# A graph network on one core: ranking work moved apart, edge sums kept in PSUM, one comparison for seven source one-hots

## The reference

```python
h = relu(layernorm(x))
# two SAGE convolutions, sums over the edges that end in a node
def conv(x, Wl, Wr, b):
    agg = segment_sum(x[src], dst); cnt = segment_sum(1, dst)
    return (agg / max(cnt, 1)) @ Wl.T + b + x @ Wr.T
x = x + conv2(relu(conv1(h)))
h = relu(layernorm(x))
# edge network, mean over the edges that START in a node
e   = relu(concat(h[src], h[dst], edge_attr) @ W1 + b1)
msg = e @ W2 + b2
out = x + segment_sum(msg, src) / max(count(src), 1)
```

## Time and profile before

| | us |
|---|---|
| median of 3 runs | 4867.47 |
| lowest, highest | 4842.37, 4877.82 |
| the profiled execution | 4839.18 |
| its span | 4837.4 |
| VectorE busy | 4073.2 (84%) |
| TensorE matmuls busy | 4006.2 (83%) |
| GpSimd busy | 2251.4 (47%) |
| ScalarE busy | 2068.5 (43%) |

### The profile page before, as it was taken

One profiled execution on the slowest core, in us unless ns is written; L12 is line 12 of the kernel. 1 busy time (PEld: TensorE's weight loads), 2 busy tenths in 40 slices (PEclk: granted clock), 3 DMA queues, 4 the chain that ended last, 5 costly groups with the idle time before them and its releaser, 6 DMA issues. The chain is left out here.

```text
span 4837.4 us, 186125 instructions
## 1 busy us (share of the span) xinstructions
PE 4006.2 (83%) x71043; PEld 3837.8 (79%) x71043; DVE 4073.2 (84%) x9221; ACT 2068.5 (43%) x4806; POOL 2251.4 (47%) x2144
## 2 busy tenths in 40 slices
PE   0788888888888899999946888888888888888886
PEld 0677778777777799999945878888888888888876
DVE  4788888888887688888876989898989898998987
ACT  1455555555554466666633222222223232232222
POOL 0000000000000466666626777777777777777771
PEclk9899999999997799999977999999989899999998
DMA  2121222222221555444414444444454455545441
GB/s 60 38 66 59 67 65 65 65 59 67 65 65 46 146 117 116 116 116 116 117 35 149 152 153 146 153 151 155 156 158 158 158 158 158 158 158 157 155 130 55
DMA packets 429135, 542.34 MB, mean 112 GB/s; under 512 B 136727, under 2 KB 393935, under 8 KB 428452
## 3 DMA queue, kind: packets, MB, share of 16 engines
q1 hardware_dynamic: 359396, 457.21, 31.0%
q0 software_dynamic: 67840, 77.39, 6.5%
q10 hardware_dynamic: 1426, 0.35, 0.0%
HBM read 462.66 MB, written 72.01 MB: 111 GB/s over the span
## 5 line engine op out<-in xcount | busy, mean ns | idle before, releaser
L1258 POOL DMA_INDIRECT sorted_edges<-edge_rows,edge_index x1590 | 1691.5, 1064 | 571.7 <-issue 476.6
L988 ACT CAST conv_rows<-conv_rows_ps 128x384 bf16<-128x384 f32 (+1 forms) x2597 | 1167.3, 449 | 873.7 <-PE conv_rows_ps L908 863.9
L908 PE MATMUL conv_rows_ps<-parts,conv_hot_t 128*128 128x192 bf16 x9328 | 1199.6, 247 | 193.3 <-DVE conv_hot_t L1052 189.9
L925 PE MATMUL conv_sums<-conv_rows,conv_hot_d 128*128 128x193 bf16 (+1 forms) x9328 | 1201.8, 247 | 4.5 <-DMA conv_got<-parts_table,conv_index 4.5
L908 PEld LDWEIGHTS conv_rows_ps<-parts,conv_hot_t 128*128 128x128 bf16 x9328 | 780.4, 98 | 238.7 <-issue 177.6
L925 PEld LDWEIGHTS conv_sums<-conv_rows,conv_hot_d 128*128 128x128 bf16 x9328 | 813.8, 98 | 5.8 <-DMA conv_got<-parts_table,conv_index 5.4
L1322 PE MATMUL edge_sums<-edge_parts,edge_hot 128*128 128x64 bf16 (+1 forms) x15582 | 588.9, 199 | 232.6 <-DVE acc L1484 232.6
L1322 PEld LDWEIGHTS edge_sums<-edge_parts,edge_hot 128*128 128x128 bf16 x15582 | 548.9, 101 | 246.3 <-DVE acc L1484 195.6
L872 POOL MEMSET acc<- 128x6500 f32 x2 | 11.0, 5514 | 1540.6 <-POOLq L440 1540.6
L886 POOL DMA_INDIRECT conv_got<-parts_table,conv_index x530 | 510.3, 963 | 291.8 <-issue 165.7
L1052 DVE TENSOR_SCALAR conv_hot_t<-conv_slot_row,node_of 128x896 bf16<-128x896 bf16 (+2 forms) x1484 | 603.5, 449 | 3.1 <-PE conv_rows_ps L908 0.8
(11 more groups left out here) (174 smaller groups left out, 4659.6 us busy)
## 6 DMA issues: line engine op xcount, KB each, us to landing
conv_slot_row<-slot_rows SPq DMA_DIRECT2D x371, 224.0 KB, 3.2
edge_slot_row<-slot_rows SPq DMA_DIRECT2D x371, 224.0 KB
edge_edges<-sorted_edges SPq DMA_DIRECT2D x371, 224.0 KB
edge_dst_row<-dst_rows SPq DMA_DIRECT2D x265, 192.0 KB
edge_attr<-in_edge_attr SPq DMA_DIRECT2D x260, 192.0 KB
conv_slot_row<-slot_rows SPq DMA_DIRECT2D x212, 192.0 KB
conv_slot_row<-slot_rows SPq DMA_DIRECT2D x159, 160.0 KB, 3.1
sorted_edges<-edge_rows,edge_index POOLq DMA_INDIRECT x1590
```

Of the source, the lines that this page charges most:

```text
L908: mm = pe.matmul(rows_ps[i % banks][:, at:at + PARTS * D], hot_t[(h + g) % 2][:, v, u * P:(u + 1) * P], k.parts[:, 2 * (GU * g + u) + v].r ...
L925: mm = pe.matmul(sums[h][:, v * wide_cols:(v + 1) * wide_cols], hot_d[(h + g) % 2][:, u, v * P:(v + 1) * P], row, start=(i == 0 and u == 0 ...
L988: act.copy(rows[i % bufs][:, 0:n, 0:PARTS * D], rows_ps[i % banks][:, 0:n * PARTS * D].rearrange("p (u d) -> p u d", u=n)).then_inc(copied, 1)
L1258: pool.indirect_dma_start(k.sorted, bass.IndirectOffsetOnAxis(ap=index[h][0:used, at:at + 1], axis=0), rows[j][0:used, t, :], None).then_i ...
```

## The change

1. **Ranking in conv1.** The instructions stay; their places in the lists change. `two_planes` is cut into two calls, one after group 2 as before and one after group 3. `choose` keeps the product after group 4; the sum (`sum_chosen`) goes behind group 5, the spreading of ranks and the first slot comparison behind group 6, and the two other comparisons behind the next block's group 0. On TensorE the first scatter piece stays at step `bs - 1`, the second and third go to steps 1 and 3 of the next block (they were at `bs - 5`, `bs - 3`, `bs - 1`), and `turn` goes from step 4 to 8. On ScalarE `take_slots` goes from step 2 to 6, `take_row` from 5 to `cut - 1`, `take_dst` from `cut - 4` to `cut - 1` (this one in conv2 too), `keep_rank` one step on.
2. **Edge sums.** `total` and `left` are gone. `add_edges`, `rest_of_first` work in place in `a_ps` (PSUM), and ScalarE's two parts and the third part read from there. `expand` waits for the third part of two groups before, where it waited for its `total`. To have a bank free, `attr_ps` has one buffer instead of two, and `turn` waits for the copy of the transpose before.
3. **Source one-hots.** The seven comparisons of `make_hot` become one, of the form that conv has for `hot_d`, with node numbers in PSUM (`nodes_ps`); `src_of` is bf16 with every number four times.

```diff
+def same_number(dve, hot, nodes, number, g):
+    shape = [P, GU, SW // QUAD, QUAD]
+    return dve.tensor_tensor(hot[:].rearrange("p u (n q) -> p u n q", q=QUAD), wide(quads(nodes), 1, shape),
+                             wide(number[:, GU * g:GU * (g + 1), :], 2, shape), ALU.is_equal)
...
 # conv, TensorE, first(b, h, n)
-                        if i == 4 and sorts(b, 1):
+                        if i in (1, 3) and sorts(b, 1):
+                            s.scatter(pe, b + 1, n if n == MANY else n + 1, (i + 1) // 2)
+                        if i == 8 and sorts(b, 1):
                             s.turn(pe, b + 1, n if n == MANY else n + 1)
 # second(b, h, n)
-                    if i in (bs - 5, bs - 3, bs - 1):
-                        s.scatter(pe, c, m, (i - bs + 5) // 2)
+                    if i == bs - 1:
+                        s.scatter(pe, c, m, 0)
...
 # conv, ScalarE
-                    if i == 2 and sorts(b, 1):
+                    if i == 6 and sorts(b, 1):
                         s.take_slots(act, b + 1, n if n == MANY else n + 1)
-                    if i == 5 and sorts(b, 1):
-                        s.take_row(act, b + 1, n if n == MANY else n + 1)
-                    if i == cut - 4 and (not isinstance(b, int) or b + 1 in range(NB)):
-                        take_dst(b + 1, 1 - h, n if n == MANY else n + 1)
                     if i == cut - 2 and sorts(b, 2):
                         s.keep_earlier(act, b + 2, n if n == MANY else n + 2)
+                    if i == cut - 1 and sorts(b, 1):
+                        s.take_row(act, b + 1, n if n == MANY else n + 1)
+                    if i == cut - 1 and (not isinstance(b, int) or b + 1 in range(NB)):
+                        take_dst(b + 1, 1 - h, n if n == MANY else n + 1)
-                    if i == bs - 4 and sorts(b, 2):
+                    if i == bs - 3 and sorts(b, 2):
                         s.keep_rank(act, b + 2)
...
 # conv, VectorE
                 if sorts(b, 2):
-                    s.two_planes(dve, b + 2, h, m)
+                    s.plane(dve, b + 2, h, m, 0)
...
+                    if g == 3 and sorts(b, 2):
+                        s.plane(dve, b + 2, h, m, 1)
                     if g == 4 and sorts(b, 2):
                         s.choose(dve, b + 2, m)
                     if g == 5 and sorts(b, 2):
-                        s.slots(dve, b + 2, m)
+                        s.sum_chosen(dve, b + 2, m)
+                    if g == 6 and sorts(b, 2):
+                        s.spread_rank(dve, b + 2)
+                        s.slots(dve, b + 2, m, 0)
...
                     make_hot(b + 1, 1 - h, n if n == MANY else n + 1, 0)
+                if sorts(b, 2):
+                    for j in range(1, PIECES):
+                        s.slots(dve, b + 2, m, j)
...
 # sum_edges
-                if n >= 1 or j >= 2:
-                    pe.wait_ge(attr_ready, q - 1)
+                if n >= 1 or j >= 1:
+                    pe.wait_ge(attr_ready, q)
...
-                pe.wait_ge(totaled, number + NG - 1)
+                pe.wait_ge(third_made, number - 1 + NG + 1)
...
-                act.activation(parts[at][:, :, 0, 0:D], total[at][:], ACT.Relu).then_inc(first_made, 1)
+                act.activation(parts[at][:, :, 0, 0:D], a_ps[at][:, 0:GU, :], ACT.Relu).then_inc(first_made, 1)
-                act.copy(parts[at][:, :, 1, 0:D], left[at][:]).then_inc(second_made, 1)
+                act.copy(parts[at][:, :, 1, 0:D], a_ps[at][:, 0:GU, :]).then_inc(second_made, 1)
...
-                dve.tensor_tensor(total[at][:], a_ps[at][:, 0:GU, :], edges[g][:], ALU.add).then_inc(totaled, 1)
+                dve.tensor_tensor(a_ps[at][:, 0:GU, :], a_ps[at][:, 0:GU, :], edges[g][:], ALU.add).then_inc(totaled, 1)
-                dve.scalar_tensor_tensor(left[at][:], total[at][:], 0.0, parts[at][:, :, 0, 0:D], ALU.max, ALU.subtract).then_inc(left_made, 1)
+                dve.scalar_tensor_tensor(a_ps[at][:, 0:GU, :], a_ps[at][:, 0:GU, :], 0.0, parts[at][:, :, 0, 0:D], ALU.max, ALU.subtract).then_inc(left_made, 1)
-                for u in range(GU):
-                    dve.tensor_scalar(hot[at][:, u, :], k.nodes_b[:], src_of[h][:, GU * g + u:GU * g + u + 1], None, ALU.is_equal)
+                same_number(dve, hot[at], nodes_ps[:, 0:SW // 2].bitcast(BF16), src_of[h], g)
-                dve.tensor_tensor(parts[at][:, :, 2, 0:D], left[at][:], parts[at][:, :, 1, 0:D], ALU.subtract).then_inc(third_made, 1)
+                dve.tensor_tensor(parts[at][:, :, 2, 0:D], a_ps[at][:, 0:GU, :], parts[at][:, :, 1, 0:D], ALU.subtract).then_inc(third_made, 1)
```

More of the change, by code:

```diff
@@ L619, in members, with plane @@
                           wide(self.number[h][:, 0], 2, shape), ALU.is_equal).then_inc(self.member_made, 1)
-    def two_planes(self, dve, c, h, n):
+    def plane(self, dve, c, h, n, i):
         shape = [P, BT, SRC_COLS // QUAD, QUAD]
-        if n >= 1:
-            dve.wait_ge(self.scattered, c)
-        dve.wait_ge(self.member_made, c + 1)
-        for i in range(2):
-            last = dve.tensor_tensor(self.planes[:, :, i, :].rearrange("p t (n q) -> p t n q", q=QUAD), self.member[:].rearrange("p t (n q) -> p t n q", q=QUAD),
-                                     wide(self.number[h][:, 1 + i], 2, shape), ALU.mult)
-        last.then_inc(self.planes_made, 1)
+        if i == 0:
+            if n >= 1:
+                dve.wait_ge(self.scattered, c)
+            dve.wait_ge(self.member_made, c + 1)
+        made = dve.tensor_tensor(self.planes[:, :, i, :].rearrange("p t (n q) -> p t n q", q=QUAD), self.member[:].rearrange("p t (n q) -> p t n q", q=QUAD),
+                                 wide(self.number[h][:, 1 + i], 2, shape), ALU.mult)
+        if i:
+            made.then_inc(self.planes_made, 1)
     def count(self, pe, c, n):
@@ L955, in first @@
                 else:
+                    for j in range(1, PIECES):
+                        if sorts(b, 1):
+                            s.scatter(pe, b + 1, n + 1, j)
                     s.count(pe, b + 2, n + 2)
@@ L1058, in make_hot @@
                     dve.wait_ge(reduced, number - 1)
-                shape = [P, GU, SW // QUAD, QUAD]
-                nodes = k.nodes_b[:] if sorting else nodes_ps[:, 0:SW // 2].bitcast(BF16)
-                dve.tensor_tensor(hot_d[hot][:].rearrange("p u (n q) -> p u n q", q=QUAD), wide(quads(nodes), 1, shape),
-                                  wide(dst_of[h][:, GU * g:GU * (g + 1), :], 2, shape), ALU.is_equal).then_inc(hot_d_made, 1)
+                same_number(dve, hot_d[hot], k.nodes_b[:] if sorting else nodes_ps[:, 0:SW // 2].bitcast(BF16), dst_of[h], g).then_inc(hot_d_made, 1)
             def take(b, h, n):
@@ L1351, in turned_back @@
                     act.wait_ge(product, q - 1)
-                act.copy(attr_t[(h + j) % 2][:], attr_ps[(h + j) % 2][:, 0:ET // 2, :]).then_inc(attr_ready, 1)
+                act.copy(attr_t[(h + j) % 2][:], attr_ps[:, 0:ET // 2, :]).then_inc(attr_ready, 1)
             def rest(b, h, n, j):
@@ L1386, in step @@
                     wait_alone(act, third_made, NG * at + 1)
[L1387 removed]
+                    act.copy(src_of[h][:], wide(k.slot_src[:, bass.ds(at, 1), :].rearrange("p b w -> p (b w)"), 2, [P, SRC_WINDOWS, QUAD])).then_inc(src_ready, 1)
             def slot(b, h, n, j):
```

31 lines of the change are left out of this document (16 added, 15 removed).

## The result

| | before | after |
|---|---|---|
| median, us | 4856.28 (4 runs) | 4629.65 (4 runs) |
| lowest, highest | 4842.37, 4877.82 | 4623.66, 4631.56 |
| the profiled execution | 4839.18 | 4631.56 |
| its span | 4837.4 | 4629.8 |

The ratio is 0.952, with a 95% interval of 0.948 to 0.956: 227 us less. I had forecast 4726 us, with a range of 4655 to 4800.

What follows compares the result with a forecast made beforehand. TensorE and VectorE stopping each other bound the first sweep, GpSimd's never-resting queue the edge sweep. 4839 - 60 (ranking) - 80 (edge sweep) = 4699 us, -2.9%, which on the 4867 median is 4726 us; range 4655 to 4800.

Steps and rivals of the forecast that it cites:

- part 4: Edge sweep, GpSimd's queue: fewer VectorE instructions with two SBUF inputs shorten issues from 1.064 to 0.98 us, 38.5 us a block.
- The sign that I gave: Edge sweep: gaps other than 0.30 us before GpSimd's issues, because the queue now waits for rows.
- parts 2, 3: Edge sweep, VectorE: one comparison of 1.09 us saves 0.37 a slot; sums in PSUM cost 0, at most 0.06 x 3.
- part 5: Edge sweep, loop of TensorE and VectorE, replayed from one turn: two blocks fall from 81.2 to 79.1 us, 39.6 a block.
- 81.2 - 2.1 = 79.1: Edge sweep: us for two blocks of TensorE's and VectorE's loop, before, saved by the change, and after.
- TensorE's slow clock at low load gives back a little: Edge sweep, slots without loads: part of VectorE's gain is lost; TensorE enters the next block only 0.8 us earlier.
- the upper of 38.5 and 39.6 sets the sweep: Edge sweep: the longer of GpSimd's queue and TensorE's loop sets the block, saving 1.5 us x 53, -80 us.
- third rival: Edge sweep: TensorE's loop is shorter than replayed, GpSimd's 38.5 us sets the block, -138 us; about 4665 in all; chance 0.15.
- So the bound passes ... to TensorE: Edge sweep: after the change TensorE, at 39.6 us a block, is the bound instead of GpSimd's queue at 38.5.
- part 1: First sweep (conv1): spreading the ranking shortens TensorE's and VectorE's stops; 1.2 us a block over 50 blocks, -60 us.
- the first sign: First sweep: a block of about 23.9 us, and TensorE's waits for the source one-hot under 2 us a block.
- second rival: First sweep: the ranking's stops only move, TensorE waits as long elsewhere; -80 to -90 us, 4784; chance 0.11.

Runs made afterwards that it cites:

- Experiment 2: The changed kernel with the edge sweep comparison's node numbers read from SBUF instead of PSUM: 4780.24 us, 0.984 of the kernel before.
- experiment 1: Parts of the change put singly into the kernel before: ranking 0.986, both edge parts 0.973, sums in PSUM 0.997, one comparison 0.993 of its time.
- experiment 4: The changed kernel with half the scatters left out, plus 32 unread small matmuls ahead of sum_up in slots without loads: 4607.44 us, two blocks 77.6 us.

## Why the prediction was right or wrong

- **GpSimd's queue (part 4): right.** 0.98 + 0.30 us an issue, 38.5 us a block; measured 0.980 + 0.305, 38.6. Experiment 2 shows the cause, experiment 1 that either VectorE change alone leaves something in its way. The sign that I gave, longer gaps because the queue would wait for rows, did not come: no gap is above 0.32 us.
- **One comparison, sums in PSUM (parts 2, 3): right.** 1.076 us for 1.09; passes in PSUM cost 2 to 6 ns more, where up to 60 were allowed for.
- **TensorE's and VectorE's loop (part 5): the step that failed.** "81.2 - 2.1 = 79.1" is 81.1 - 3.4 = 77.7. The mis-sized term is the gain in slots with loads. I let TensorE's 5.24 us a slot bind in all of them and wrote "the rest up to the turn ... stay", but VectorE comes out of every stretch without loads behind TensorE, and goes at its own 5.07 until it has caught up; the last two slots alone gave 0.7 where I had nothing, the five ahead of them 0.8 where I had 0.5. And "TensorE's slow clock at low load gives back a little" took away a gain that was there: by the fifth add it was 1.6 us, not 0.8 (0.5 of them behind the turn already). Against these stand 0.6 us lost at the turn, which I had unchanged. With this, "the upper of 38.5 and 39.6 sets the sweep" picked the wrong loop. The sweep gave 2.6 us a block, (41.19 - 38.59) x 51 = 133 us, not 80. That is the third rival, TensorE's loop shorter than replayed; of its reason, the clock, experiment 4 and VectorE's waits leave some 0.2 to 0.3 us a pair.
- **"So the bound passes ... to TensorE": wrong.** The queue never waits (no gap above 0.32 us), yet with half of its issues gone the block stays as long: the two loops are tied within 0.5 us a pair, and neither alone is the bound.
- **The ranking (part 1): right in kind, small by a quarter.** I worked out 1.34 us a block and took 1.2; measured 1.64, and -83 us against -60. VectorE still waits 0.8 us a block for the reduce, where I had written that it no longer would. With the prefix earlier, where TensorE's list is the bound, the block is 22.9 us and not the 21.9 that I had for TensorE's own work (its 3.24 us of stops hold 0.2 more than the rows show, TensorE's wait for a copy of ranks). TensorE's waits for the source one-hot are 0.8 us a block, as the first sign asked (under 2). The second rival falls.
- **The base.** I scaled to the median of the runs shown. The sum on the profiled execution was 4839 - 60 - 80; with the measured terms it is 4839 - 83 - 134 = 4622, and the projections' levels (+27, -14) and conv2 (-4) make 4631. So scaling to the median, +27 us on the forecast, went the wrong way too.
- **The chances.** I gave 0.82 to faster by over 1%, and it was; but the rival that comes nearest had 0.15. The range ended at 4655 since it let only one of two independent terms come out large; both did.

## What to carry to other kernels

Where two loops are within a few per cent of each other, cost a change for each loop by itself, and give the sweep the larger of the two; and replay slot by slot which engine is behind, since an engine that comes out of a short stretch late runs at its own pace, not at the leader's. Ask of a GpSimd queue of indirect DMAs that never rests what its single issues overlap: moving one operand of one VectorE instruction to PSUM was worth 2.3 us of a 41 us block here, at no change in VectorE's own time. And when one wait is cut and another stands untouched in the same loop (the copied ranks), it is the next thing to move.

## What the runs showed of the hardware that I had not expected

**Two levels of the same f32 matmuls, and of the clock.** The projection ahead of the first sweep, 196 matmuls, unchanged code; groups by line, 100 to 260 us, before, then after:

```profile
L523 PE MATMUL conv_in_rows_ps<-conv_w,conv_in_h_t 64*128 64x128 f32 x196 | 25.6, 281 | 0.0
```

```profile
L531 PE MATMUL conv_in_rows_ps<-conv_w,conv_in_h_t 64*128 64x128 f32 x196 | 46.6, 428 | 0.0
```

With the prefix earlier it was 279 ns. There are four such projections, and each differs from one execution to the next: ahead of the first sweep (281 or 428 ns, 27 us), ahead of conv2 (428 ns before; in after the clock came back within it, 345 ns, which is the -14), ahead of the edge sweep (279 or 428 ns, 25 us) and behind it (274 or 413 ns, 26 us). The level is the clock's. The last projection in the kernel before, 4800 to 4820 us, and with the ranking alone, 4760 to 4780 us (busy us and count of PE, PEld, DVE, ACT, POOL; granted clock, DMA share, GB/s):

```profile
4800.00:4820.00 20.00, 19.86 (x180) 19.53 (x180) 12.47 (x24) 7.62 (x9) 0.00 (x0) 1.00 0.31 80
```

```profile
4760.00:4780.00 20.00, 20.00 (x98) 20.00 (x97) 6.85 (x13) 3.65 (x4) 0.00 (x0) 0.50 0.22 57
```

At 1.00, which is the 2.4 GHz level, 180 matmuls go through in 20 us, at 0.50, the 1.2 GHz level, 98. Ahead of conv2 the kernel before has a granted clock of 0.50 from 1530 us on and the same 428 ns. Ahead of the first sweep the profile gives 1.00 for both levels, but the trace of after has no record of the clock before 217 us, so that this 1.00 is no measurement there. Each of the four is worth 14 to 27 us, 0.3 to 0.6% of the time, in code that nobody changed, and they ride on every median above. What decides whether the clock comes back within a projection is open.

**GpSimd's gap.** Between two indirect DMAs there are 0.305 us in every kernel in which the queue never waits, whatever the issue takes (0.979 to 1.064 us in the mean).
